# First sum's statistics on ScalarE, residual added by VectorE, third unit's quantisation and last turns reordered

## The reference

```
x = x + tanh(g_xattn[0]) * pruned_attention(layernorm(x), ctx)      # 16 heads of 16
x = x + tanh(g_ffn[0])   * fp4_ffn(layernorm(x))                    # 256 -> 704 -> 256
x = x + tanh(g_xattn[1]) * linear_attention(ctx, layernorm(x))      # ends in its own layernorm
x = x + tanh(g_ffn[1])   * int8_linear(layernorm(x))                # 256 -> 256
```

## Time and profile before

| | us |
|---|---|
| median of 3 runs | 1242.76 (1242.36 to 1247.11) |
| the profiled execution's own time | 1247.91 |
| its span | 1246.2 |
| PE busy | 1027.6 (82%) |
| DVE busy | 1022.0 (82%) |
| ACT busy | 917.3 (74%) |
| mean granted TensorE clock | 0.967 |

### The profile page before, as it was taken

One profiled execution on the slowest core, in us unless ns is written; L12 is line 12 of the kernel. 1 busy time (PEld: TensorE's weight loads), 2 busy tenths in 40 slices (PEclk: granted clock), 3 DMA queues, 4 the chain that ended last, 5 costly groups with the idle time before them and its releaser, 6 DMA issues.

```text
span 1246.2 us, 17959 instructions
## 1 busy us (share of the span) xinstructions
PE 1027.6 (82%) x5720; PEld 493.9 (40%) x5720; DVE 1022.0 (82%) x2041; ACT 917.3 (74%) x2031; POOL 159.2 (13%) x167
## 2 busy tenths in 40 slices
PE   6888999977777777777777777898999999999984
PEld 5655566511111111111111112336667666666652
DVE  5887677788888898889888886347989999999965
ACT  4456656489999999999999995664466656655644
POOL 2231230020000000000000001001212131213122
PEclk9899999989999999999999998898999999999987
DMA  9630562042212022221203201011011111110001
GB/s 300 173 112 1 197 160 102 3 118 44 44 32 42 21 40 43 44 45 33 42 19 73 44 19 52 9 40 29 26 35 36 59 43 34 42 53 27 18 18 34
DMA packets 77890, 71.80 MB, mean 58 GB/s; under 512 B 13738, under 2 KB 71396, under 8 KB 77796
## 3 DMA queue, kind: packets, MB, share of 16 engines
q1 hardware_dynamic: 77796, 70.65, 21.3%
HBM read 42.83 MB, written 27.28 MB: 56 GB/s over the span
## 4 chain that ended last, share of the span: by engine, by line
PE 42%; ACT 36%; DVE 10%; issue 9%; SPq 1%; DMA 1%; POOL 0%; DVEq 0%; ACTq 0%
ACT ea L1318 18%; ACT prob L1332 15%; PE ps_a L1574 11%; PE ps_b L1532 6%; PE ps_c L1547 3%; PE ps_v L1532 2%; DVE nmax L1219 2%; PE ps_a L1583 1%; PE ps_v L1191 1%; PE ps_c L1676 1%; PE ps_a L1554 1%; PE ps_b L756 1%; PE ps_b L1142 1%; PE ps_c L1175 1%; PE ps_b L731 1%
## 5 line engine op out<-in xcount | busy, mean ns | idle before, releaser
L1318 ACT ACTIVATE ea<-ps_a,nmax 128x512 f32<-128x512 f32 x512 | 362.9, 748 | 68.1 <-DVE nmax L1219 68.1
L1219 DVE TENSOR_REDUCE nmax<-ps_a 128x2 f32<-128x1024 f32 x256 | 313.6, 1225 | 52.9 <-PE ps_a L1142 51.6
L1332 ACT ACTIVATE prob<-ps_b 128x1024 f32<-128x1024 f32 x214 | 236.3, 1104 | 0.0
L1142 PE MATMUL ps_b<-q_st,k_st 52*128 52x512 f16 x512 | 106.6, 393 | 136.8 <-ACT prob L1332 128.1
L1142 PEld LDWEIGHTS ps_b<-q_st,k_st 52*128 52x128 f16 x512 | 26.3, 93 | 365.5 <-ACT prob L1332 303.6
L1574 PE MATMUL ps_a<-wgu,xT 128*128 128x352 f32 x512 | 164.5, 466 | 2.7 <-ACT xT L1707 2.3
L1191 PE MATMUL ps_v<-prob,v_in 128*16 128x512 f32 x1024 | 136.7, 606 | 11.6 <-DVE att L1286 11.6
L1175 PE MATMUL ps_c<-ea,rz 128*32 128x512 f32 x1024 | 138.1, 612 | 0.0
L1318 ACT ACTIVATION_READ_ACCUMULATOR ea<-ps_a,nmax 128x1 f32 x512 | 136.1, 266 | 0.0
L1719 ACT ACTIVATE ea<-ps_a 128x352 f32<-128x352 f32 x128 | 59.5, 466 | 77.7 <-PE ps_a L1574 77.7
L1574 PEld LDWEIGHTS ps_a<-wgu,xT 128*128 128x128 f32 x512 | 94.5, 192 | 50.5 <-issue 5.2
(11 more groups left out here) (272 smaller groups left out, 1682.2 us busy)
## 6 DMA issues: line engine op xcount, KB each, us to landing
k_scr<-k_p SPq DMA_DIRECT2D x24, 256.0 KB, 2.9
q_scr<-q_p SPq DMA_DIRECT2D x24, 256.0 KB, 2.8
q_st<-q_scr SPq DMA_DIRECT2D x32, 192.0 KB, 4.7
k_st<-k_scr SPq DMA_DIRECT2D x32, 192.0 KB, 5.0
c_in<-in_ctx SPq DMA_DIRECT2D x8, 512.0 KB, 4.5
x_in<-in_x SPq DMA_DIRECT2D x8, 512.0 KB, 6.5
v_scr<-v_s SPq DMA_DIRECT2D x8, 512.0 KB, 3.3
v_in<-v_scr SPq DMA_DIRECT2D x16, 256.0 KB, 3.1
```

The lines of the kernel that those rows point to most:

```text
L1142: return e.matmul(bank, left[b][o:o + rows, r, t * P:t * P + P], right[b][o:o + rows, r], start=True, stop=True)
L1219: e.tensor_reduce(nmax[u % 2][:, t].rearrange("p (h r) -> p r h", h=2)[:, r], ps_a[:, z % 2 * 2:z % 2 * 2 + 2], AX_X, ALU.max, negate=True ...
L1318: e.activation(ea[c % RING][:, g % 4], ps_a[:, g % 4], ACT.Exp, bias=nmax[u % 2][:, t, n:n + 1], accum_out=tot[u % 2][:, t, n:n + 1]).then ...
L1332: e.activation(dst, ps_b[:, :, :], ACT.Exp).then_inc(s_prob, 1)
```

## The change

ScalarE computes mean (`first_mean`: Copy with scale 1/256 and accumulated sum) and the sum of squared deviations (`first_squares`: Square of mean minus x) of the first sum, for unit i+1 in turn i. VectorE's `first_stats` is gone, and `variances_a` becomes two instructions, the second of which waits for the squares. The identity matmul is gone; the first projection chunk of each tile starts its accumulation, tile 0 in one bank of `ps_b` and tile 1 in the other, for all units. `residual` on VectorE adds r1 to it and writes r2 to SBUF, which the statistics, the decoder's normalisation and `rb` read. Unit 2 is quantised in the attention's tail, and its turn is called with `opened=True`; some pieces of units 0 and 1 move by one step. In turns from 16 on ScalarE treats the decoder before z and its transposed copy before the hidden one, TensorE in turn 16 takes the decoder's transpose and product first, and VectorE in turn 16 takes `roots_b` between the two rounding instructions. The last unit's int8 product is made in two banks, with output and store for each tile. Cut to its core:

```diff
+            parts = N if u5 == UNITS - 1 else 1            # SyncE: store of u5
+            for t in range(parts):
+                o, n = t * N // parts, N // parts
+                e.wait_ge(s_dve_out, u5 + 1 + t)
+                e.dma_start(tokens(out[j, p * U + o * P:p * U + (o + n) * P]), o_b[p][:, o:o + n])...
...
# TensorE
     def down(u, r):
+            if r == 0:
+                if u == 0:
+                    e.wait_ge(*at.weighted)
+                e.wait_ge(s_dve_r2, u)
+            return products(d_ps, ..., (2 * r, 2 * r + 1), r == 2, r == 0, True)
     def turn(i, opened=False):
+            if last:                                       # last = i == UNITS
+                decoder_T(u2, i)
+                decoder_product(u2)
...
-            if u2 is not None:
+            if u2 is not None and not last:
+                decoder_T(u2, i)
...
-                e.matmul(d_ps[u1 % 2], ident[:, :], flat(r1[u1 % 3][:, :, :]), start=True,
-                         stop=False).then_inc(s_pe_sum, 1)
...
-            if u2 is not None:
+            if u2 is not None and not last:
+                decoder_product(u2)
...
# ScalarE
+        def first_mean(u):
+            e.wait_ge(s_dve_r1, u + 1)
+            if u:
+                e.wait_ge(s_nb_a, u)
+            for t in range(N):
+                ins = e.activation(sq[:, t], r1[u % 3][:, t], ACT.Copy, scale=1.0 / D, accum_out=mv_a[:, 0, t, 0:1])
+            ins.then_inc(s_act_st1, 1)
+
+        def first_squares(u):
+            e.wait_ge(s_act_st1, 2 * u + 1)
+            if u:
+                e.wait_ge(s_ve_a, u)
+            for t in range(N):
+                ins = e.activation(sq[:, t], r1[u % 3][:, t], ACT.Square, scale=-1.0, bias=mv_a[:, 0, t, 0:1],
+                                   accum_out=mv_a[:, 0, t, 1:2])
+            ins.then_inc(s_act_st1, 1)
     def turn(i, opened=False):
                 for q in range(3):
                     leave(u0, q)
+            if i >= UNITS and u2 is not None:
+                decoder(u2, i)
             if u3 is not None:
                 ...normal(z, pairs(y_ps), rs_b[p], nb_b[p], 1)
             if u0 is not None:
                 leave(u0, 3)
+            if unit(i + 1) is not None:
+                first_mean(i + 1)
+            if u0 is not None:
                 leave(u0, 4)
+            if u2 is not None and i < UNITS:
+                decoder(u2, i)
             if u0 is not None:
                 leave(u0, 5)
+            if i >= UNITS and u2 is not None:
+                decoder_T(u2)
             if u1 is not None:
                 hidden_T(u1, 0)
+            if unit(i + 1) is not None:
+                first_squares(i + 1)
+            if u2 is not None and i < UNITS:
+                decoder_T(u2)
# VectorE
+        def residual(u):
+            e.wait_ge(s_pe_down, u + 1)
+            e.wait_ge(s_act_dec, u)
+            e.tensor_tensor(r2[:, :, :], at.ps_b[:, :, 0:D], r1[u % 3][:, :, :], ALU.add).then_inc(s_dve_r2, 1)
+            e.wait_ge(s_dve_r2, u + 1)
         def variances_a(i):
-            e.wait_ge(s_dve_st1, min(i + 1, UNITS))
-            e.tensor_scalar(ve_a[i % 2][:, :, :], mv_a[:, :, :, 1], LN_EPS, None, ALU.add).then_inc(s_ve_a, 1)
+            e.tensor_scalar(ve_a[i % 2][:, 1], mv_a[:, 1, :, 1], LN_EPS, None, ALU.add).then_inc(*dv.up())
+            e.wait_ge(s_act_st1, 2 * min(i + 1, UNITS))
+            e.tensor_scalar(ve_a[i % 2][:, 0], mv_a[:, 0, :, 1], 1.0 / D, LN_EPS, ALU.mult, ALU.add).then_inc(s_ve_a, 1)
         def round_blocks(q, mag, g, between=None):
+            if between is not None:
+                roots_b(between)                           # between the two roundings, in turn 16
# run: the attention's tail, n = z - tail
 TensorE:  x_T(0) at 18 -> 19, gate_or_up(0, ...) from 19 -> 20
 ScalarE:  + first_mean(0) 8, first_squares(0) 9, first_mean(1) 15, first_squares(1) 16,
           + first_mean(2) 35, first_squares(2) 36, x_normal(2) 40, x_magnitude(2) 42
           x_normal(0) 13 -> 14, x_magnitude(0) 16 -> 17, x_T(0) 19 -> 20, leave(0, ...) 20 -> 21, gate(0) 28 -> 29
 VectorE:  - first_stats; variances_a(0) 8 -> 10, roots_a(0) 11 -> 12, x_start(0) 14 -> 15, x_round(0) 17 -> 18
           + variances_a(2) 37, roots_a(2) 39, x_start(2) 41, x_round(2) 43
 ScalarE and VectorE: turn(2, opened=True), then turn(i) from 3 on
```

More of the change, by code:

```diff
@@ L1414, in feed @@
     tr = [at.ps_a[:, 2 + n] for n in range(2)]
-    d_ps = [at.ps_b[:, n] for n in range(2)]
+    d_ps = [at.ps_b[:, n, 0:D] for n in range(N)]
     w_ps, y_ps = at.ps_c[:, :], at.ps_v[:, :]
@@ L1441, in unit, with out_ps @@
         return n if 0 <= n < UNITS else None
+    def out_ps(u, t):
+        return (y_ps if u == UNITS - 1 and t else w_ps)[:, t * D:t * D + D]
     def flat(x):
@@ L1527, in tensor, with products @@
     def tensor(e):
[L1528 removed]
+        def products(dst, left, right, chunks, last=True, first=False, apart=False):
             for t in range(N):
                 for c in chunks:
[L1532 to L1533 removed]
+                    ins = e.matmul(dst[t], left(c, t), right(c), start=(first and c == chunks[0]),
+                                   stop=(last and (apart or t == N - 1) and c == chunks[-1]))
             return ins
@@ L1734, in hidden_T, with decoder, decoder_T, turn @@
             ins.then_inc(s_act_hT, 1)
-        def turn(i):
+        def decoder(u, i):
+            p = i % 2
+            e.wait_ge(s_nb_b, i + 1)
+            e.wait_ge(s_pe_decT, u)
+            normal(dec, r2, rs_b[p], nb_b[p], 0).then_inc(s_act_dec, 1)
+        def decoder_T(u):
+            e.wait_ge(s_pe_decT, u + 1)
+            e.wait_ge(s_pe_y, u)
+            e.activation(decT[:, :, :].rearrange("p c t -> p (c t)"), tr[0], ACT.Copy).then_inc(s_act_decT, 1)
+        def turn(i, opened=False):
             u0, u1, u2, u3, u4, u5 = (unit(i - d) for d in range(6))
@@ L1952, in turn @@
                 e.wait_ge(*dv.now())
-            if i < TURNS_A:
+            if i < TURNS_A and not opened:
                 variances_a(i)
@@ L1979, in turn @@
                 h_start(u1)
-            if u0 is not None:
+            if u0 is not None and not opened:
                 x_start(u0)
@@ L1990, in turn @@
             if u1 is not None:
-                h_round(u1)
-            if i < TURNS_B:
+                h_round(u1, UNITS if i == UNITS else None)
+            if i < TURNS_B and i != UNITS:
                 roots_b(i)
@@ L2188, in _ @@
                     h_magnitude(0)
+                if n == 35:
+                    first_mean(2)
+                if n == 36:
+                    first_squares(2)
                 if 33 <= n < 41:
                     leave(1, n - 33, plain=True)
+                if n == 40:
+                    x_normal(2)
+                if n == 42:
+                    x_magnitude(2)
             gate(1)
             hidden_T(0, 0)
-            for i in range(2, fd.turns):
+            turn(2, opened=True)
+            for i in range(3, fd.turns):
                 turn(i)
@@ L2262, in _ @@
                     first_sum(2)
-                    first_stats(2)
                 if n == 37:
+                    variances_a(2)
                     roots_b(1)
                     h_scaled(0)
-            for i in range(2, fd.turns):
+                if n == 39:
+                    roots_a(2)
+                if n == 41:
+                    x_start(2)
+                if n == 43:
+                    x_round(2)
+            turn(2, opened=True)
+            for i in range(3, fd.turns):
                 turn(i)
```

162 lines of the change are left out of this document (82 added, 80 removed).

## The result

The changed kernel takes **1251.06 us** (median; 1250.70 to 1252.31) beside 1242.76 of the kernel before: a ratio of 1.0056, 95% interval [1.0033, 1.0079]. The forecast was 1240, range 1231 to 1250; the kernel is slower by a little over the 0.5% that can be told from no change, and outside the range. The profiled execution has a span of 1249.5 us, own time 1251.23. Three executions in what follows ran in a slower state of the chip (one each of b_early3, a_early_squares and the kernel before) and are left out of the ratios.

A forecast was written before the change was run, and what follows sets the result against it. TensorE was taken as the bound, with VectorE only 0.62 us slack per turn. Steady turns -2.0, third unit's move 0 and last turns -0.5 gave -2.5 us from 1242.76: forecast 1240 us, range 1231 to 1250.

The forecast's parts named there:

- TensorE's share: Steady feed turn: the identity product goes, 0.86 us of 24.77, leaving 23.91 us by TensorE alone.
- VectorE's share: Steady feed turn: statistics -0.94, residual add +0.72, variances +0.10; VectorE's own turn goes from 24.15 to about 24.03 us.
- The new wait in a steady turn: VectorE waits 0.4 to 0.5 us for ScalarE's squares before the variances; turn 24.57 us, ten turns -2.0 us.
- The rival without a wait: Squares come in time, VectorE bounds the steady turn at 24.03 us: -7.4 us, 1235 us in all; chance 0.20.
- The third unit's move: Unit 2 quantised earlier, in VectorE's idle hole at the feed stage's start: 0, ends -5.2 and +5.6 us.
- The statistics between exponentials: Means and squares of three units among attention exponentials: 5.6 us of ScalarE, 2.3 counted as uncovered.
- The clock rival: TensorE idles 1.24 us per steady turn and its clock falls: 1248 us, or 1255 in all ten; chance 0.22.
- The last turns: New order and split last product at the end: sum -0.5 us, ends -3 and +2.
- Carrying over: The -2.5 us from the profiled execution, 5.15 us above the median, applied to the median 1242.76: 1240.3 us.
- Table loads: Rival: Square not in Exp's table, so three calls among exponentials bring loads, 5 us counted: 1245 us; chance 0.08.
- Dear statistics: Rival: ScalarE's mean and squares cost more, steady turn 25.1 us, +3.3 - 0.5: 1246 us; chance 0.10.

The follow-up runs named there:

- b_early3: The kernel before with only the third unit's quantisation moved forward; 1241.28 us, 0.9972 of the kernel before.
- a_early_squares: The changed kernel with ScalarE's squares moved to just behind the fifth product's drain, ahead of the decoder's normalisation; 1241.84 us, 0.9978 of the kernel before.
- a_res_only: The changed kernel with the first sum's statistics back on VectorE at their old places; 1239.54 us, 0.9968 of the kernel before.
- b_again: The kernel before, unchanged, profiled a second time; span 1241.6 us, median 1246.82 us over twelve executions.

## Why the prediction was wrong

**TensorE's share and VectorE's share** (23.91 and 24.03 us): right within 0.1. The identity rows are gone, and with the wait removed the turn is 23.95.

**The new wait in a steady turn** (squares end 11.3 us behind the first product's start, wait 0.4 to 0.5, turn 24.57, -2.0 in all): right. They end 11.3 us behind it (1014.32 - 1003.05); VectorE came a little earlier than worked out and waits 0.70, and yet the turn is 24.45 and ten of them give -2.8. The rival without a wait, -7.4 us, is what a_early_squares measured there: 247.6 - 239.8 = 7.8.

**The step that failed: the statistics on ScalarE were priced in the ten steady turns alone.** Ahead of them the sum has one term of 0, which measured +9.5 us: +4.0 in turns 2 to 4, by the wait, and +5.5 in the opening (below). The forecast says that the variances stand in VectorE's queue ahead of all that TensorE's next turn needs, and yet costs the same wait at nothing where the turns differ. In turn 2 VectorE has no sums and outputs of older units, so it comes to the variances 7.7 us behind the first product's start (857.64 - 849.91) instead of 10.4, while ScalarE's squares end 11.2 behind it, as late as ever, behind a drain tied to TensorE. It waits 3.30 us. In turns 3 and 4 it waits 1.59 each: it is early there too (idle 1.97 and 1.79 us for z just before), and the squares are later, 13.4 us behind the product in turn 3, since the matmuls ahead of them begin at half clock. In turns 2 and 3 GpSimd's root adds 0.90 us, TensorE stands 3.4 us each time, and the products behind run at half clock. With everything of the change but the statistics, turns 2 to 4 take 71.8 us (a_res_only), with them 79.1: they cost 7.3, and the other parts give back 3.3, hence the net +4.0. With only their place moved (a_early_squares) it is 71.3, so it is the place of the squares that costs and not their being on ScalarE. The forecast noted that these turns are bound by VectorE and drew from it only that a gain would be lost.

**The third unit's move** (0, ends -5.2 and +5.6): as a part of this change 0 within the measurement (1.0062 against 1.0065), and TensorE's idle time did move ahead of the projection, 3.27 us. Alone it gains 0.28%, in turn 2. The 0 for this part came out by luck: two errors cancel, the gain that I missed and the wait that I missed.

**The statistics between exponentials** (2.3 us counted, inside that 0): the opening took 5.5 us more, and ScalarE's own time is little of it. Missing were unit 0's chain one attention step later, in the diff but priced nowhere, about 2.4 us, and TensorE's clock, about 3 us; why the clock is low there in every profile of the changed kernel stays open. The clock rival looked for a fall in the middle turns, where the clock stayed at 1.00 from 925 to 1173 us.

**The last turns** (-0.5): +0.3 in the profile, and nothing that the time can tell.

**Carrying over** from an execution 5 us above the median: legitimate only if its extra time is outside what changes. About 3 us of it were the clock fall at 755 us, which the changed kernel has in every profile. So 3 of the 8.3 us between the medians were already in the rows that the sum was made against, and the difference could only look small there: 1249.5 - 1246.2 = 3.3 on the spans, 7.9 against b_again.

**Rivals.** Table loads: excluded. ScalarE's timeline in the changed kernel has the squares straight between exponentials:

```profile
754.43 1.08 ACT L1329 ACTIVATE prob<-ps_b 128x512 f32<-128x512 f32 x2
755.38 0.52 ACT L1727 ACTIVATE sq<-r,mv_a 128x256 f32<-128x256 f32 x1
...
756.27 0.21 ACT L1727 ACTIVATION_READ_ACCUMULATOR sq<-r,mv_a 128x1 f32 x1
756.37 1.09 ACT L1329 ACTIVATE prob<-ps_b 128x512 f32<-128x512 f32 x2
```

From 740 to 840 us there are three loads, as before, all for Silu and back. The Trainium skill (ScalarE: Activation LUTs, Table sets: the hidden batching unit) names no set for Square; here it runs beside Exp without a load. Dear statistics: no, 1.11 us for the squares and 0.80 for the mean until the next could start, against 1.06 and 0.75.

## What to carry to other kernels

A wait that moves to another engine has to be priced in every phase that runs the same code: the first turns have the same queue with less in it, so the engine arrives earlier and waits longer. Place the producer by the earliest consumer, and ahead of work that is itself tied to a third engine: three entries of the queue earlier was worth 0.8% here, two later cost 2.6%. Price the parts of a change together as well as apart: in turns 2 to 4 the other parts gave 3.3 us back alone, and cost 2.5 beside the statistics. Before a difference is carried from a profiled execution to a median, find where that execution was slow.

## What the hardware showed

- Two profiles of one kernel differ by 3 us from FP to unit 0's transpose (24.93 and 21.93) because TensorE's granted clock fell in one of them in the window from 755 to 760 us and held at 1.00 in the other, among attention steps in which TensorE waits 0.49 to 1.07 us for exponentials.
- A 128x256 Square with a pointer bias took 0.53 us and its read 0.22, two with their reads 1.11 us from start to end; the mean, a Copy with a sum, 0.43 and 0.21, two with reads 0.92.
- In the changed kernel, TensorE's waits of 0.7 to 0.9 us ahead of the transpose and 0.18 behind it, in every steady turn, left the granted clock at 1.00; behind the three waits of 3.27, 3.42 and 3.48 us it was at 0.50 to 0.53.
- Square ran between exponentials without a table load.
